# Values projected token by feature, with rows shifted one partition by DMA, in place of values projected feature by token and transposed

## The reference, cut to what matters

```python
qkv = hidden @ W_pack
v = qkv[..., NH * HD + NKV * HD:].reshape(b, s, NKV, HD)
v = _causal_conv2(v, conv_v)        # w[g,0] * v[token-1] + w[g,1] * v[token]; token -1 is zero
v = jnp.repeat(v, group, axis=2)
...
out = jnp.einsum('bhqk,bkhd->bqhd', probs, v).reshape(b, s, NH * HD)
```

## Time and profile before

| | us |
|---|---|
| median of 3 runs | 759.4 (758.58 to 760.25) |
| the profiled execution, its own time | 758.73 |
| its span in the profile | 756.9 |

### The profile page before, as it was taken

The page is one execution under the profiler, slowest core; times in us unless marked ns, Lnnn a source line. Parts: engine busy times, 40 slices in busy tenths (PEclk is TensorE's granted clock), DMA queues, the critical chain, the costliest instruction groups (busy, mean ns, idle before and its releaser), DMA issues.

```text
span 756.9 us, 12875 instructions
## 1 busy us (share of the span) xinstructions
PE 731.7 (97%) x4144; PEld 622.0 (82%) x4144; DVE 530.8 (70%) x1554; ACT 466.7 (62%) x1275; POOL 428.5 (57%) x337
## 2 busy tenths in 40 slices
PE   8799999999999999999999999999989999999997
PEld 7598889988899998889999888999867767777775
DVE  5898897689876868987686797778655224464374
ACT  5788868777986776798677678777553212222110
POOL 3545445454465588646558865655534527577356
PEclk9999999999999999999999999999998999999999
DMA  8960007600005011000501102050369669996762
GB/s 301 325 137 1 2 1 243 225 1 2 1 1 194 2 48 48 33 1 1 167 2 48 47 22 77 2 168 1 124 174 262 216 212 294 287 241 72 171 225 84
DMA packets 62418, 84.44 MB, mean 112 GB/s; under 512 B 6376, under 2 KB 50293, under 8 KB 62352
## 3 DMA queue, kind: packets, MB, share of 16 engines
q1 hardware_dynamic: 52240, 70.59, 30.1%
q0 software_dynamic: 7680, 8.95, 6.2%
q10 hardware_dynamic: 2432, 4.07, 1.5%
HBM read 54.81 MB, written 33.51 MB: 117 GB/s over the span
## 4 chain that ended last, share of the span: by engine, by line
PE 80%; DVE 11%; ACT 5%; issue 2%; DMA 1%; POOL 0%; ACTq 0%; DVEq 0%; POOLq 0%
PE PJ L1376 22%; PE OUT L1510 9%; PE U L1495 6%; PE U L1455 6%; PE U L1658 5%; PE U L1484 4%; PE OUT L1607 3%; PE U L1607 3%; PE U L1454 3%; PE U L1496 3%; PE U L1376 3%; PE OUT L1677 2%; PE XB L1677 2%; PE XB L1376 2%; ACT U L567 1%
## 5 line engine op out<-in xcount | busy, mean ns | idle before, releaser
L788 POOL TENSOR_TENSOR qsw<-qsw,sinT 128x512 f32<-128x512 f32 x95 | 125.5, 1321 | 167.6 <-ACT qsw L554 166.7
L1008 DVE CUSTOM_DVE_ANT_0 U<-U,mask 128x128 f32<-128x128 f32 (+1 forms) x256 | 86.6, 380 | 50.7 <-PE U L1455 50.3
L567 ACT ACTIVATE U<-U,nmax 128x128 f32<-128x128 f32 (+1 forms) x256 | 100.4, 393 | 32.2 <-DVE nmax L1008 31.7
L1376 PE MATMUL PJ<-hT_hi,w_hi 128*128 128x512 f32 x254 | 110.8, 436 | 1.1 <-issue 1.1
L1376 PE MATMUL PJ<-hT_lo,w_hi 128*128 128x512 f32 x254 | 100.4, 395 | 0.0
L1376 PE MATMUL PJ<-hT_hi,w_lo 128*128 128x512 f32 x254 | 100.1, 394 | 0.0
L792 POOL TENSOR_TENSOR qr<-qr,qsw 128x512 f32<-128x512 f32 x64 | 82.5, 1289 | 29.1 <-DVE qr L992 28.6
L799 POOL DMA_INDIRECT slot_rows<-xn,sidx x64 | 64.4, 1007 | 48.6 <-issue 13.7
L553 ACT ACTIVATE qsw<-PJ 64x512 f32<-64x512 f32 x96 | 57.0, 594 | 51.8 <-PE PJ L1376 42.4
L1510 PE MATMUL OUT<-wo_hi,oT_hi 128*128 128x256 f32 x256 | 82.9, 324 | 1.4 <-DVE wo_lo L1032 1.2
L1025 DVE TENSOR_TENSOR oT_lo<-U,oT_hi 128x256 fp32r<-128x256 f32 x128 | 54.2, 423 | 40.7 <-ACT oT_hi L574 40.5
(11 more groups left out here) (224 smaller groups left out, 1839.5 us busy)
## 6 DMA issues: line engine op xcount, KB each, us to landing
wgu<-in_dram SPq DMA_DIRECT2D x32, 352.0 KB, 9.7
expert_sum<-blank SPq DMA_DIRECT2D x3, 2176.0 KB, 17.5
slot_rows<-blank SPq DMA_DIRECT2D x1, 4624.0 KB, 26.4
late_sums<-expert_sum SPq DMA_DIRECT2D x9, 512.0 KB, 8.8
wd_a<-in_dram SPq DMA_DIRECT2D x12, 352.0 KB
wraw<-in_dram SPq DMA_DIRECT2D x8, 512.0 KB, 9.0
bcm<-mod_rows SPq DMA_DIRECT2D x8, 512.0 KB, 6.7
xe<-slot_rows ACTq DMA_DIRECT2D x10, 289.0 KB, 6.8
```

The costliest lines, as they stand in the source:

```text
L567: last = act.activation(U[n % 3][:, a:z], U[n % 3][:, a:z], ACT.Exp, scale=-1.0, bias=nmax[:, n % 4, j:j + 1], accum_out=rsum[:, n % 4, j: ...
L788: pool.tensor_tensor(pair3(qsw[:, n % NQSW, :]), pair3(qsw[:, n % NQSW, :]), both(sinT[:, :]), ALU.mult).then_inc(t2_done, 1)
L1008: last = dve.tensor_tensor_reduce(out=U[n % 3][:, a:z], in0=U[n % 3][:, a:z], in1=allowed, scale=-float(HD) ** -0.5, scalar=3.4e38, op0=AL ...
L1376: last = pe.matmul(out_ap, a(c), b_(c), start=(n == 0), stop=(n == len(steps) - 1))
```

## The change: v is projected token by feature

The operands of the v matmuls change places: the normalised input, 128 tokens of it, becomes the stationary operand, and the weights of two groups (256 columns) the moving one. The result has tokens on the partitions already: one turn gives 2 blocks of 128 tokens (one batch) x 256 features (two groups), again a bank of 128x512. There are again 32 v turns, each now of twelve matmuls of 128x256 instead of six of 128x512. `v_transpose` and `v_rows` are gone.

The token before is now the partition above. ACT writes the bank times the first tap (two activations, one for each group) to a `qsw` slot; three DMAs, issued by SP, carry its rows one partition further to a new tile `vsh`: 112 partitions, 15 partitions, and one (the last row of the first 128 tokens goes to the first row of the second 128). DVE writes the bank times the second tap to `vN`, and POOL adds `vsh` (`earlier_token`).

The list of projections is now `TURNS`: k, q, v, q for each group, with v(G+1) in group G, since one v turn serves two groups for one batch; the first group has both v turns 0 and 1, five turns in all. LEAD is 5, so that k and q stand at the same steps as before. A `qsw` slot is now taken by every turn, v as well; a slot is free again for the turn three later when its rope is done, or, after a v turn, when its three DMAs have landed (`ld_vsh`). The SP program becomes a loop over the v turns, `next_tokens(v)` first; the blanks are cut into 8 and 9 pieces and spread over the turns, and the pair loads and stores are put at fixed turns. `yg` now shares its memory with `xnT_lo`.

```diff
-LEAD = 4
-W_ORDER = (4, 0, 6, 1, 5, 2, 7, 3)
+LEAD = 5
+W_ORDER = (4, 0, 6, 1, 7, 5, 2, 3)
...
+NV = NU // 4
+
+TURNS = []
+for _G in range(NU // 4):
+    TURNS += [("k", _G, 0), ("q", _G, 0)]
+    TURNS += [("v", v, 0) for v in ((0, 1) if _G == 0 else (_G + 1,)) if v < NV]
+    TURNS += [("q", _G, 1)]
...
-        v0 = sb("v0", [PN, 2, S + 1], F32, att)
         kc = sb("kc", [PN, 2, TOK], F32, att)
-        vT = sb("vT", [PN, TOK], F32, att)
-        vN = sb("vN", [PN, 2, TOK], F32, att)
+        vN = sb("vN", [PN, 2, 2, 2, 2 * HD], F32, att)
+        vsh = sb("vsh", [PN, 2, 2, 2 * HD], F32, att)
...
+        gated_rows = ExitStack()
+        yg = sb("yg", [PN, 2, 2, H], F32, gated_rows)
+        gated_rows.close()
         xnT_lo = sb("xnT_lo", [PN, HC, TOK], F32R, att)
-        yg = sb("yg", [PN, 2, 2, H], F32, att)
...
-            sp.wait_ge(fills, 9)
-            sp.dma_start(slots_d.rearrange("(s e) h -> s e h", e=E), blank[:, :].unsqueeze(1).broadcast_to([PN, E, ROW])).then_inc(st_zero, 16)
-
-            sp.wait_ge(mod_done, 1)
-            sp.dma_start(mod_d, mod[:, :]).then_inc(st_mod, 16)
-            sp.wait_ge(st_mod, 16)
+            def next_tokens(v):
+
+                u = TURNS.index(("v", v, 0))
+                rows_v = qsw[:, u % NQSW, :].rearrange("p (t c) -> p t c", t=2)
+                sp.wait_ge(pj_act, u + 1)
+                if v >= 2:
+                    sp.wait_ge(v_done, v - 1)
+                for to, part, at, src in ((16, PN, slice(0, 2), slice(0, 2)), (1, 16, slice(0, 2), slice(0, 2)), (0, 1, slice(1, 2), slice(0, 1))):
+                    rows_from = slice(to - 1, part - 1) if to else slice(PN - 1, PN)
+                    sp.dma_start(vsh[to:part, v % 2, at, :], rows_v[rows_from, src, :]).then_inc(ld_vsh[v % 2], 16)
...
+            def blank_slots(k):
+                four = slice(4 * k, 4 * (k + 1))
+                sp.dma_start(slots_d.rearrange("(s e) h -> s e h", e=E)[:, four, :],
+                             blank[:, :].unsqueeze(1).broadcast_to([PN, 4, ROW])).then_inc(st_zero, 16)
...
+            sp.wait_ge(fills, 9)
+            for v in range(NV):
+                p, at = divmod(v, GROUPS)
+                next_tokens(v)
+                if 1 <= v <= 8:
+                    blank_slots(v - 1)
+                if v == 7:
+                    mod_store()
+                    pair_loads(0)
+                if 9 <= v < 9 + 3 * NSUM:
+                    blank_sums(v - 9)
+                if at == 5 and p + 2 < NPAIR:
...
+                if v == NV - 4:
+                    shared_weights()
+                if p > 0 and at == 7:
+                    pair_stores(p - 1)
+                if p > 1 and at == 0:
+                    pair_loads(p - 1)
+            pair_loads(LAST)
...
+                if u >= NQSW:
+                    if TURNS[u - NQSW][0] == "v":
+                        v = TURNS[u - NQSW][1]
+                        act.wait_ge(ld_vsh[v % 2], 48 * (v // 2 + 1))
+                    else:
+                        act.wait_ge(rope_done, rope_number(u - NQSW) + 1)
+                if kind == "v":
+
+                    for g in range(2):
+                        tap = 2 * (i // 2 * 2 % GROUPS + g)
+                        heads = slice(g * HD, (g + 1) * HD)
+                        last = act.activation(qsw[:, slot, :].rearrange("p (t c) -> p t c", t=2)[:, :, heads],
+                                              bank[:, :].rearrange("p (t c) -> p t c", t=2)[:, :, heads], ACT.Copy,
+                                              scale=cwv[:, tap:tap + 1])
+                    last.then_inc(pj_act, 1)
                     return
...
-
-            def v_rows(G):
-                act.wait_ge(vt_ps, G + 1)
-                if G >= 2:
-                    act.wait_ge(pv_ps, 4 * (G - 1))
-                act.activation(vN[:, G % 2, :], XB[:, :], ACT.Copy).then_inc(vn_done, 1)
...
+            def earlier_token(u):
+
+                if TURNS[u][0] != "v":
+                    return
+                v = TURNS[u][1]
+                pool.wait_ge(ld_vsh[v % 2], 48 * (v // 2 + 1))
+                pool.wait_ge(pj_dve, u + 1)
+                pool.tensor_tensor(v_tile(v), v_tile(v), vsh[:, v % 2, :, :], ALU.add).then_inc(v_done, 1)
...
-                    dve.scalar_tensor_tensor(pair3(vT[:, :]), pair3(PJ[m % 2][:, :]), cwv[:, 2 * g + 1:2 * g + 2],
-                                             v0[:, :, 0:S], ALU.mult, ALU.add).then_inc(pj_dve, 1)
...
+                if kind == "v":
+
+                    if i >= 4:
+                        dve.wait_ge(pv_ps, 8 * (i // 2 - 2) + 7 + i % 2)
+                    g = i // 2 * 2 % GROUPS
+                    tap = cwv[:, 2 * g + 1:2 * g + 4:2].unsqueeze(1).unsqueeze(3).broadcast_to([PN, 2, 2, HD])
+                    dve.tensor_tensor(v_tile(i).rearrange("p t (g d) -> p t g d", g=2),
+                                      PJ[u % 2][:, :].rearrange("p (t g d) -> p t g d", t=2, g=2), tap,
+                                      ALU.mult).then_inc(pj_dve, 1)
...
+                    if p > 0:
+                        dve.wait_ge(st_xnt, 32 * p)
...
+                if kind == "v":
+
+                    for t in range(2):
+                        tk = slice(i % 2 * S + t * PN, i % 2 * S + (t + 1) * PN)
+                        last = halves(PJ[u % 2][:, t * 2 * HD:(t + 1) * 2 * HD], HC,
+                                      ((lambda c: hT_hi[:, p % 2, c, tk], lambda c: hT_lo[:, p % 2, c, tk]), weights))
+                else:
+                    last = halves(PJ[u % 2][:, :], HC,
+                                  (weights, (lambda c: hT_hi[:, p % 2, c, :], lambda c: hT_lo[:, p % 2, c, :])))
+                last.then_inc(pj_ps, 1)
...
-            def v_transpose(G):
-
-                p, g = divmod(G, GROUPS)
-                pe.wait_ge(pj_dve, 4 * G + 3)
...
-                for j in range(TT):
-                    last = pe.transpose(XB[:, j * PN:(j + 1) * PN], vT[:, j * PN:(j + 1) * PN], ident[:, :])
-                last.then_inc(vt_ps, 1)
...
-                if n % 4 == 0:
-                    pe.wait_ge(vn_done, G + 1)
+                if G % 2 == 0 and n % 4 < 2:
+                    pe.wait_ge(v_done, G + b + 1)
                 o = U[n % 3][:, 0:S]
-                v = vN[:, G % 2, b * S:(b + 1) * S]
-
-                pe.matmul(o, v[:, 0:PN], pT[:, n % 2, 0:S], start=True, stop=False)
-                pe.matmul(o[:, PN:S], v[:, PN:S], pT[:, n % 2, S:S + PN], start=False, stop=True).then_inc(pv_ps, 1)
+                v = vN[:, G // 2 % 2, b, :, G % 2 * HD:(G % 2 + 1) * HD]
```

More of the change, by code:

```diff
@@ L39 @@
 LCOL = 64
-LEAD = 4
-W_ORDER = (4, 0, 6, 1, 5, 2, 7, 3)
+LEAD = 5
+W_ORDER = (4, 0, 6, 1, 7, 5, 2, 3)
 WC = QKV // 8
-W_FREE = NU - UNITS // 2
+W_FREE = NU - UNITS // 2 + 1
 SW_PARTS = 4
@@ L254, in adaln_block @@
             sem(n) for n in ("var1", "rstd1_done", "xhat_done", "ht_ps", "ht_used", "h_hi_done", "h_lo_done"))
[L256 to L257 removed]
+        pj_ps, pj_act, pj_dve, t2_done, rope_done, k0_done, kc_done, v_done = (
+            sem(n) for n in ("pj_ps", "pj_act", "pj_dve", "t2_done", "rope_done", "k0_done", "kc_done", "v_done"))
         sc_ps, sneg_done, exp_done, rinv_done, norm_done, pt_ps, pt_done, pv_ps, ot_done = (
@@ L302, in adaln_block, with columns, w_chunks @@
         WO_PART = NH // len(WO_STEPS)
-        def head_of(l):
-            g = l // 4
-            return (NH + g, 2 * g, NH + NKV + g, 2 * g + 1)[l % 4]
-        def w_chunks(l):
-            return W_ORDER.index(head_of(l) * HD // WC) + 1
+        def columns(u):
+            kind, i, h = TURNS[u]
+            g = i % GROUPS
+            first = {"k": (NH + g) * HD, "q": (2 * g + h) * HD, "v": (NH + NKV) * HD + (g // 2) * 2 * HD}[kind]
+            j, at = divmod(first, WC)
+            return j, slice(at, at + (2 * HD if kind == "v" else HD))
+        def w_chunks(u):
+            return W_ORDER.index(columns(u)[0]) + 1
         def x_pair(p):
@@ L325, in ht_scaled, with rope_number, rope_buffer, v_tile @@
             return HC * p + c + (p == 0)
-        def rope_number(m):
-            return 3 * (m // 4) + ROPE_OF[m % 4]
-        def rope_buffer(m):
-            g, r = m // 4, m % 4
-            return kr[:, :] if r == 0 else qr[:, 0 if r == 1 else 1, g % 2, :]
+        def rope_number(u):
+            return sum(kind != "v" for kind, _, _ in TURNS[:u])
+        def rope_buffer(u):
+            kind, G, h = TURNS[u]
+            return kr[:, :] if kind == "k" else qr[:, h, G % 2, :]
+        def v_tile(v):
+            return vN[:, v // 2 % 2, v % 2, :, :]
         def later(n):
@@ L678, in _ @@
             for n in STEPS:
-                if 0 <= n - 1 < NU and n % 4 == 1:
-                    v_rows(n // 4)
-                if 0 <= n + 3 < NU:
-                    project(n + 3)
+                if 0 <= n + LEAD - 1 < NU:
+                    project(n + LEAD - 1)
                 if 0 <= n - 2 < NU:
@@ L772, in _ @@
```

(30 more changed lines are left out.)

140 lines of the change are left out of this document (55 added, 85 removed).

## The result

The changed kernel takes 766.05 us (median of 9 executions, 761.7 to 771.2), the one before 759.4 (9 executions, 757.1 to 762.9). The ratio is 1.0081, with a 95% interval from 1.0061 to 1.0101: slower by 0.8%. The forecast was 753.0. The profiled execution took 766.05 itself, with a span of 764.2 us.

A forecast was written before the change was run, and what follows sets the result against it. PE was taken to bound the kernel, through attention without any other engine between. 758.7 - 14.1 + 1.3 + 4.6 + 2.0 + 0.5 = 753.0 us; own range 749 to 757, 8 in 10 for 746.5 to 757.5.

The forecast's parts named there:

- Transposes and matmuls: v turns on PE: removing 32 groups' transposes saves 14.1 us; twelve matmuls of 128x256 instead of six cost 1.3 us.
- The start: First steps: first shift queues behind weight loads until 34.0, delaying scores, +4.6 us; POOL/DVE meetings and lower clock, +2.0.
- Steady state: Every group after the start: shift DMAs hidden, POOL's 1.28 us addition fits its idle gap exactly, cost 0.
- Rival 3: Every group: POOL's addition and DVE block each other, pushing a rope into k_conv; slower, 770 us at half price; chance 0.10.
- Rival 2: Steps with scatters: POOL falls behind 1.2 us a group, k or q miss their scores, 756 us; chance 0.13.
- Rival 1: Start: first shift passes the weight loads, lands at 28, so the start costs nothing, 746 us; chance 0.12.
- rival 4: v turns: the twelve matmuls cost more than 0.12 us each; at 0.153 the saving is gone, about 766; chance 0.05.
- Ends of the pairs: Three stretches of some 12 us where DVE is nearly full: PE's saving partly not passed on, +0.5 us.
- The pieces of the blanks: SP's DMAs between v turns: each piece, at most 0.8 MB, has 15 us until the next v turn, cost nothing.

The follow-up runs named there:

- the last comparison: Kernel before with DVE's wo_lo and gate bound moved and post_x1 split, 759.1 us, against changed kernel with these edits, mended start and DVE's addition from third v turn, 748.1.
- the second profile: One more profile of the changed kernel with nothing altered, to see whether the falls of the granted clock recur; 763.2 us.

## Why the prediction was wrong

- *Transposes and matmuls, -14.1 + 1.3.* Right: 3.74 instead of 4.19 us in every fourth step, twelve matmuls in 1.42. The 11.0 us of the last comparison are close to these 12.8.
- *The start, +4.6 + 2.0.* Mechanism and times right (34.0 forecast, 33.84 found; 38.1 and 37.73), size too low: 8.4 us instead of 6.6. `scores(4)` was 8.05 us late, and the clock stood at 0.50 for the four microseconds after the gap. Issued ahead of the last 2 MB of loads, the shift let POOL add at 28.56 instead of 33.84. The Trainium skill has the rule that the prediction drew on in DMA: Bandwidth & Descriptors, Queues, rings and completion order: each DMA engine takes the descriptors of a queue in ring order. By that rule the shift gains by standing further ahead, and these 5.3 us agree. The range's lower end is loose: the bounds that the prediction gives lead to 751, not 749.
- *Steady state, "it fits exactly, cost 0".* This is the step that failed: the term was 0, and some 11 us stand in its place (11.2 by the medians above). It asked only whether POOL has 1.28 us free, and whether `k_conv` would be met. POOL had the time, and `kc` didn't suffer (0.96 us on average, 0.99 before). But it never listed what DVE runs in that gap. Cut to two columns, the addition gives 10.6 us back, 2 of them in the start; put into the kernel before, it costs 4.6. Shown are two ways: it meets DVE's `wo_lo`, `xin` and the gate's bound in the first pair (3.1 to 4.8 us came back by moving two `wo_lo` and the bound), and it makes POOL late behind the scatters, so that PE waits 2.6 and 2.3 us for `kc`, of which 1.0 us each is left when the wait that goes away is counted. A third comes on top in some executions: the granted clock falls behind such a wait, 0.61 at 74 to 78 us in the first profile and 1.00 there in the second. In steps, the second profile loses 2.5 us at 8 to 11, 2.1 at 20 to 23, 2.0 at the two pair ends and 2.7 in the groups from steps 40, 44, 72, 76 and 120, each of which fails to win its 0.45; with the addition cut short these five win it. How the 11.2 us divide isn't settled to better than some 2 us, as the clock varies from execution to execution. At steps 9 to 10 the addition isn't the only cause: PE waits 1.47 us there with two columns, too, and what else brings the meeting about wasn't tried apart from moving `wo_lo`.
- *Rival 3* named the mechanism, with 0.10, and priced it at the wrong instruction (its sign, `k_conv` well over 0.74 us in many groups, didn't come: half of them took 0.744 us or less in both kernels). The Trainium skill states it more widely than I used it (SBUF — State Buffer, Who interferes with whom): besides DVE instructions with two SBUF inputs, `tensor_scalar` in a two-port mode blocks and is blocked. `xin`, a `tensor_scalar` with one tensor in SBUF, agrees: 1012 ns on average with the addition and 722 with two columns of it.
- *Rival 2* (POOL late at the scatters, +3 us) was real as a wait, but taken away it gave no time, as another wait came back. *Rival 1* fell with the shift at 33.84, *rival 4* with 0.12 a matmul.
- *Ends of the pairs, +0.5*: not measured alone; what the steps show there is in the 11.2 us above. The pieces of the blanks at nothing: right as far as waits go. PE waited for no DMA that it hadn't waited for before (`ident` 2.7 us, `wm` 0.4), and POOL waited for `vsh` only at the start, 9.9 us.

## What to carry to other kernels

Work that is put into an engine's gap must be held against what the other engines run in that gap, instruction by instruction, not against the gap's length and one critical instruction. In a stream with no idle time, an added instruction of 1.3 us on a side engine can cost nearly as much as the work saved on the main one (11.2 against 12.8 us here), and part of that can be had back by moving its neighbours by one step. A wait that disappears in one place may only have hidden another: look at the lateness step by step, not at the waits alone.

## What the runs showed of the hardware

A DVE instruction on 8 partitions is held up until POOL's large one is over: four rows of the kernel after, DVE and then POOL.

```profile
122.53 1.27 DVE L1006 TENSOR_SCALAR gabs<-gabs 8x256 f32<-8x256 f32 x1
123.84 1.26 DVE L1007 TENSOR_SCALAR gsgn<-mod 8x256 f32<-8x256 f32 x1
...
122.18 1.48 POOL L845 TENSOR_TENSOR vN<-vN,vsh 128x512 f32<-128x512 f32 x1
123.61 1.34 POOL L832 TENSOR_TENSOR qsw<-qsw,sinT 128x512 f32<-128x512 f32 x1
```

Each of the two ends 0.14 to 0.15 us behind POOL's. In the kernel before the same two took 0.28 us each. A DMA of 224 KB from SBUF to SBUF landed 2.5 us after its issue (median of 32). Beside the weight loads, issued on another queue than theirs, a shift of three DMAs took 7.6 us from its first issue to the end of POOL's wait. And the granted clock fell behind the router matmuls in some executions of a kernel and not in others, without any wait of PE before it.
